# Sparse feed-forward: an expert's second bias is loaded as one row and spread over the partitions by GpSimd, not by the DMA

## What is computed

```python
D, H, E, K, C = 256, 1024, 64, 3, 128          # features, hidden, experts, choices, capacity
def _L0_ffn_ref(x, gate_w, gate_b, w1, b1, w2, b2):
    xf = x.reshape(-1, D)
    logits = xf @ gate_w + gate_b
    top_l, top_i = jax.lax.top_k(logits, K)
    gates = jax.nn.softmax(top_l, axis=-1)
    # each token goes to its 3 experts; an expert keeps its first 128 tokens
    buf = jnp.zeros((E, C, D), x.dtype).at[fe, pos].set(xf[tok], mode='drop')
    h = jax.nn.gelu(jnp.einsum('ecd,edh->ech', buf, w1) + b1[:, None, :], approximate=False)
    y = jnp.einsum('ech,ehd->ecd', h, w2) + b2[:, None, :]
    rows = y[fe, jnp.minimum(pos, C - 1)] * (fg * valid.astype(x.dtype))[:, None]
    return jnp.zeros_like(xf).at[tok].add(rows).reshape(x.shape)

x = x + 0.5 * _L0_ffn_ref(_layernorm(x), ...)   # twice, around attention 0
```

## Time and profile before

| what | us |
|---|---|
| median of 3 runs | 3428.24 (3416.62 to 3428.94) |
| the profiled execution | 3400.82 |
| its span | 3398.8 |
| PE busy | 2905.2 (85%) |
| PE weight load busy | 2080.4 (61%) |
| DVE busy | 1733.6 (51%) |
| ACT busy | 1579.4 (46%) |
| POOL busy | 1286.1 (38%) |
| q1 (SP's DMAs) | 413.98 MB, 47.3% of the 16 engines' span |
| q0 (POOL's DMAs) | 33.57 MB, 4.6% |

### The profile page before, as it was taken

How to read it: one execution, slowest core, us unless ns; L and a number is a source line. 1 busy time by engine, 2 the same in 40 slices (tenths; PEclk the granted TensorE clock), 3 DMA queues, 4 the chain that set the end, 5 groups by cost and what they waited for, 6 DMA issues and landing times. The chain is left out here.

```text
span 3398.8 us, 56446 instructions
## 1 busy us (share of the span) xinstructions
PE 2905.2 (85%) x20629; PEld 2080.4 (61%) x20629; DVE 1733.6 (51%) x4827; ACT 1579.4 (46%) x2598; POOL 1286.1 (38%) x1215
## 2 busy tenths in 40 slices
PE   3599999958999998555999997899859999998997
PEld 3488888823444443345988886566536666665665
DVE  4711111158888788266111111577656666665665
ACT  1133333239988889121333332233237777783332
POOL 3423333359998888043333332000133343320000
PEclk8699999979999999556999999899879999998999
DMA  7179999822554444451999997100066544631001
GB/s 258 44 231 325 317 320 319 264 63 23 59 77 67 58 63 58 49 178 38 296 321 321 315 319 241 37 0 0 19 95 95 81 70 74 90 45 29 0 0 49
DMA packets 368922, 450.78 MB, mean 133 GB/s; under 512 B 87316, under 2 KB 325671, under 8 KB 363559
## 3 DMA queue, kind: packets, MB, share of 16 engines
q1 hardware_dynamic: 344102, 413.98, 47.3%
q0 software_dynamic: 24576, 33.57, 4.6%
HBM read 380.90 MB, written 66.58 MB: 132 GB/s over the span
## 5 line engine op out<-in xcount | busy, mean ns | idle before, releaser
L1542 ACT ACTIVATE f_h_t<-f_h_ps,f_b_t 128x128 f32<-128x128 f32 x1024 | 319.6, 363 | 662.3 <-PE f_h_ps L1501 662.3
L1908 POOL TENSOR_TENSOR a_dmg_buf<-a_c 128x2048 f32<-128x2048 f32 x128 | 520.0, 4087 | 70.8 <-PE a_dmg_ps L1955 45.8
L1501 PEld LDWEIGHTS f_h_ps<-f_rows_t,f_w 128*128 128x128 f32 x4096 | 482.7, 194 | 9.9 <-issue 3.5
L1501 PE MATMUL f_h_ps<-f_rows_t,f_w 128*128 128x128 f32 x4096 | 483.8, 277 | 2.3 <-DVE f_rows_t L1554 1.2
L1512 PE MATMUL f_y_ps<-f_w,f_h_t 128*128 128x256 f32 x2048 | 462.9, 379 | 0.0
L1470 POOL DMA_INDIRECT acc_rows<-f_y,f_give x128 | 203.1, 1587 | 641.7 <-DMA acc_rows<-f_y,f_give 490.1
L1512 PEld LDWEIGHTS f_y_ps<-f_w,f_h_t 128*128 128x128 f32 x2048 | 379.3, 190 | 46.4
L2240 DVE SCALAR_TENSOR_TENSOR a_bond_buf<-a_a,a_small_rep,a_q_ps 128x512 f32<-128x512 f32 x512 | 346.9, 740 | 38.4 <-PE a_bond_ps L1955 36.7
L420 DVE SCALAR_TENSOR_TENSOR f_acc<-f_y_ps,f_gate,f_acc 128x256 f32<-128x256 f32 x576 | 246.5, 479 | 138.0 <-PE f_y_ps L309 132.5
L860 ACT ACTIVATE a_prob<-a_prob,a_neg_top 128x128 f32<-128x128 f32 (+3 forms) x512 | 274.7, 561 | 60.6 <-POOL a_neg_top L674 60.1
L957 DVE CUSTOM_DVE_ANT_0 a_prob<-a_s_ps,a_factor 128x128 f32<-128x128 f32 (+3 forms) x512 | 235.5, 487 | 105.8 <-PE a_s_ps L751 102.4
(11 more groups left out here) (307 smaller groups left out, 4325.8 us busy)
## 6 DMA issues: line engine op xcount, KB each, us to landing
f_w<-in_L_ffn_w_dram SPq DMA_DIRECT2D x256, 1024.0 KB, 7.6
f_b<-in_L_ffn_b_dram SPq DMA_DIRECT2D x128, 128.0 KB, 9.7
a_skewed<-skew SPq DMA_DIRECT2D x8, 2048.0 KB, 8.5
a_q_s<-parts SPq DMA_DIRECT2D x64, 256.0 KB, 10.8
a_k_s<-parts SPq DMA_DIRECT2D x64, 256.0 KB
parts<-a_parts SPq DMA_DIRECT2D x32, 384.0 KB, 7.8
acc_rows<-x_resid SPq DMA_DIRECT2D x17, 512.0 KB, 4.5
xn_rows<-f_xn SPq DMA_DIRECT2D x16, 512.0 KB, 3.1
```

The lines of the kernel that those rows point to most:

```text
L1501: last = nc.tensor.matmul(h_ps[n // HB][:, (n % HB) * P:(n % HB + 1) * P], w1_sb[s][:, c, n * P:(n + 1) * P], rows_t[e % 2][:, c, :], star ...
L1542: nc.scalar.activation(h_t[k][:, n, :], h_ps[n // HB][:, (n % HB) * P:(n % HB + 1) * P], ACT.Gelu, bias=b1_t[:, n, e:e + 1]).then_inc(gelu ...
L1908: nc.gpsimd.tensor_tensor(dmg_buf[n % RING][:, :, :], places(c_sb[h], first_place(dg)), c_sb[h][:, PAD:].unsqueeze(1).broadcast_to([P, DG, ...
```

## The change

SP loads the bias of an expert into one partition, [1, 256]. GpSimd writes it to all 128 partitions with its operation `partition_broadcast`, into one of two buffers [128, 256], one expert ahead of its use. DVE waits for it with a new semaphore, `b2_spread`.

```diff
-        b2_sb = [sb(f"b2_{s}", [P, D]) for s in range(R)]
+        b2_row = [sb(f"b2_row{s}", [1, D]) for s in range(R)]
...
         def load_weights(sp, s, e):
             sp.dma_start(w1_sb[s][:, :, :], w1[e, :, :].rearrange("(c p) h -> p c h", p=P)).then_inc(w_loaded[s], 16)
             sp.dma_start(w2_sb[s][:, :, :], w2[e, :, :].rearrange("(c p) d -> p c d", p=P)).then_inc(w_loaded[s], 16)
-            sp.dma_start(b2_sb[s][:, :], b2[e:e + 1, :].rearrange("o d -> (o d)").partition_broadcast(P)).then_inc(w_loaded[s], 16)
+            sp.dma_start(b2_row[s][:, :], b2[e:e + 1, :]).then_inc(w_loaded[s], 16)
...
+        b2_sb = [sb(f"b2_{k}", [P, D]) for k in range(2)]
...
+            def spread_bias(e):
+                pool.wait_ge(w_loaded[e % R], (e // R + 1) * 48)
+                if e >= 2:
+                    pool.wait_ge(y_copied, e - 1)
+                nc.gpsimd.partition_broadcast(b2_sb[e % 2][:, :], b2_row[e % R][:, :]).then_inc(b2_spread, 1)
+
             for e in range(R):
                 gather(e)
+            spread_bias(0)
             pool.wait_ge(acc_stored, 16 * B)
             for e in range(E):
+                if e + 1 < E:
+                    spread_bias(e + 1)
                 add_rows(e)
                 if e + R < E:
                     gather(e + R)
...
             def finish(e):
                 k = e % 2
                 dve.wait_ge(y_ready, e + 1)
-                nc.vector.tensor_tensor(y_biased[k][:, :], y_ps[k][:, 0:D], b2_sb[e % R][:, :], ALU.add)
+                dve.wait_ge(b2_spread, e + 1)
+                nc.vector.tensor_tensor(y_biased[k][:, :], y_ps[k][:, 0:D], b2_sb[k][:, :], ALU.add)
```

More of the change, by code:

```diff
@@ L1069, in load_weights @@
             sp.dma_start(w2_sb[s][:, :, :], w2[e, :, :].rearrange("(c p) d -> p c d", p=P)).then_inc(w_loaded[s], 16)
-            sp.dma_start(b2_sb[s][:, :], b2[e:e + 1, :].rearrange("o d -> (o d)").partition_broadcast(P)).then_inc(w_loaded[s], 16)
+            sp.dma_start(b2_row[s][:, :], b2[e:e + 1, :]).then_inc(w_loaded[s], 16)
         route(core, sparse, name, gate_w, gate_b, E, b1, b1_rows, b1_loaded, take, give, gate, xn_stored, acc_stored,
               load_weights, R)
-        experts(core, sparse, name, E, H, R, b1_rows, b1_loaded, w1_sb, w2_sb, b2_sb, take, give, gate, acc_stored,
+        experts(core, sparse, name, E, H, R, b1_rows, b1_loaded, w1_sb, w2_sb, b2_row, take, give, gate, acc_stored,
                 w_loaded, load_weights)
@@ L1411, in _, with experts @@
             read_table()
-def experts(core, sparse, name, E, H, R, b1_rows, b1_loaded, w1_sb, w2_sb, b2_sb, take, give, gate, acc_stored,
+def experts(core, sparse, name, E, H, R, b1_rows, b1_loaded, w1_sb, w2_sb, b2_row, take, give, gate, acc_stored,
             w_loaded, load_weights):
@@ L1441, in experts @@
         gelu_done = sem("gelu_done")
+        b2_spread = sem("b2_spread")
         y_ready = sem("e_y_ready")
```

## The result

The changed kernel takes **3378.39 us** (median of 4 runs, 3377.82 to 3381.95), the kernel before 3422.61 in the same series (4 runs, 3416.62 to 3428.94): ratio 0.9873, 95% interval 0.9848 to 0.9898, 44 us or 1.3% faster. The forecast of 3412 was too high by 34 us, and the time lies 6 us under the range.

What follows compares the result with a forecast made beforehand. The expert loop was taken as bound by gathers standing behind weight loads, with PE's 7.24 us as floor. Bias -20, broadcast 0 and switch +3.4 gave -16.6 us: 3412 us from the median 3428.24, range 3384 to 3438.

Steps and rivals of the forecast that it cites:

- What bounds the kernel: Expert loop, two passes: PE waits for late gathers only, 28 times in 55 experts; 7.79 us an expert.
- the floor: Expert loop: PE's own time for an expert, 7.24 us, below which the period cannot fall.
- The 66 us of the prediction: Expert loop: all that cheaper transfers can win, 33 us a pass over 60 experts.
- POOL's transfers behind the load: Expert loop: POOL's small transfers on q0 stand behind a whole load on q1, whose last part is the bias.
- The bias leaves the load: Expert loop: 128 packets fewer, 0.37 us of queue, 0.18 us an expert; 20 us won, bounds 0 and 41.
- the half: Expert loop: shortening a load by d shortens the period by d/2, because the loop spans two experts.
- The count of 55 limited steps: Expert loop: some 55 limited steps a pass, 110 in all, since first four and last few experts are excluded.
- rival 1: Expert loop: the bias counts in full, each scatter landing 0.37 us sooner; 41 us won, 3391 us; chance 0.15.
- The broadcast at nothing: POOL in the expert loop: a broadcast takes 1.26 us, hidden in idle time before scatters; cost 0.
- The switch: GpSimd's code switched around the passes: 6 us each, hidden except 3.4 us exposed at attention 0.
- The base: Whole kernel: gain taken from 3428.24 us, median of runs shown, not the profiled execution's 3400.8.
- Rivals 2, 3 and 4: Nothing won in the loop, 3432 us (0.25); long code switches, slower, 3446 (0.09); slow broadcast bounds POOL, 4068 (0.03).

Runs made afterwards that it cites:

- early_load: Changed kernel with a small IOTA behind each pass's last scatter and SP issuing loads once the down product is done and the row spread: 0.9812, 3356.65 us.
- bias_distinct: Kernel before, but from the fifth expert of each pass the spread bias load is replaced by 128 different 1 KB rows of the second weight: 0.9934.
- w2_less: Kernel before with its spread bias, but from the fifth expert of each pass the last 128 rows of the second weight are not loaded: 0.9904.
- bias_wide: Kernel before, but from the fifth expert of each pass the spread bias load is replaced by 128 KB in 32 rows of 4 KB: 0.9961.
- w_early: Kernel before, but SP issues an expert's two weights once the down product is done, and only the bias waits for VectorE's read: 0.9916.
- first_four: Kernel before, but the spread biases of each pass's first four experts are issued at the end of the route phase, not its head: 0.9979.
- row_plain: Changed kernel without the broadcast on GpSimd; the bias add reads two tiles set to zero once: 0.9858, 3371.07 us.
- bias_twice: Kernel before with the spread bias loaded a second time, into an unread tile, from the fifth expert of each pass: 1.0269, 3513.4 us.
- before_again: Kernel before, unchanged, run for a second profile: 0.999, span 3420.4 us.
- early_again: Changed kernel with one small IOTA into an unread tile behind each pass's last scatter, run beside the changed kernel on one chip: 0.9847, 3374.73 us.
- w2_runs: Changed kernel with small IOTA, second weight laid out as one 8 KB run per partition, first weight read with stride 8: 1.1261, 3855.53 us.

## Why the prediction was wrong, point by point

- **What bounds the kernel: right in the main.** The gather is the only DMA that PE waits for, and 7.24 us is the floor: 28 waits became 8, and early_load with one wait runs at the floor. The 66 us of the prediction are about what is to be had; the changed kernel took 39 us and early_load 59 (966.3 - 906.9).
- **POOL's transfers behind the load: still so.** In the changed kernel a scatter is issued at 403.07 us; from 403.5 to 405.5 all packets are of q1, from 405.5 to 407.5 726 are q1's and 4 q0's, and from 407.5 to 409.5 q0 moves 186:

```profile
q1 hardware_dynamic: 392, 0.77, 100.7%
```

```profile
q1 hardware_dynamic: 726, 0.74, 108.3%
q0 software_dynamic: 4, 0.00, 1.3%
```

```profile
q0 software_dynamic: 186, 0.25, 58.7%
q1 hardware_dynamic: 80, 0.12, 41.0%
```

  The Trainium skill (DMA: Bandwidth & Descriptors, "Queues, rings and completion order") would have them alternate; by these rows they do not, in the changed kernel either. POOL's packets come through as a load runs out.
- **The bias leaves the load: the term that failed.** The sum took 0.37 us of queue and let a step keep half, 0.18 us, 20 us in all; 0.31 us a step was measured, 39.3 us. The picture behind the half was wrong. The prediction saw one load in the period of two experts, "from about 351.0 to 357.0". But SP issues a load in each step, and the first profile shows it in the same stretch:

```profile
340.79 0.37 SPq L1068 DMA_DIRECT2D f_w<-in_L_ffn_w_dram  x1
...
349.27 0.37 SPq L1068 DMA_DIRECT2D f_w<-in_L_ffn_w_dram  x1
...
356.57 0.37 SPq L1068 DMA_DIRECT2D f_w<-in_L_ffn_w_dram  x1
```

  The load issued at 340.79 holds POOL's transfers back as well. The scatter of 344.31 and the gather of 346.21 had been issued; from 345.5 to 348.0 us all packets are q1's, and from 348.5 to 350.5 q0 moves 161:

```profile
q1 hardware_dynamic: 828, 0.92, 107.6%
```

```profile
q0 software_dynamic: 161, 0.22, 49.5%
```

  So two loads stand in the 15.3 us, and both became shorter. Two times 0.37 us, less what the floor of 7.24 cuts off, would give the measured 0.62 us for two steps. That is an argument and not a measurement, for no run times the bias in the queue by itself, and another reading fits too: a spread bias that costs more than 0.37 us, of which a step keeps about half. bias_distinct speaks for it: its 128 different rows cost 0.18 us a step more than the changed kernel (7.54 against 7.36), just what the prediction had taken, and the one row read 128 times adds 0.13. w2_less, with 0.25 us for 128 KB, lies between. Shown is that the term was 0.31 and not 0.18, and that each step has a load of its own; how much of the miss lies in the half and how much in the price of the transfer stays open.
- **The count of 55 limited steps and rival 1.** All 63 intervals of a pass together gave 19.1 and 20.2 us, so the count did little. Rival 1's 41 us come close to the 39.3; it had 0.15. Whether they come about as it said, with each scatter 0.37 us sooner, no run shows. The evidence against it, that PE waits at every second turn only, says where a delay shows and not how many loads it comes from.
- **What the 0.31 us is made of.** Leaving out 128 KB of the second weight gives 0.25 us (w2_less); the row read 128 times costs 0.13 us more than 128 different ones (bias_distinct); packets as such cost little (bias_wide, 0.05). These don't add up exactly; the floor may cut each. The lag ahead of the issue counts too: 0.88 us of it gave 0.19 us a step (w_early), where a full count would have reached the floor.
- **Four biases less in the route phases: not considered, and not settled.** The changed kernel has 2.6 and 1.0 us less there by the table, and first_four 3 to 4 us in the second, but other profiles speak against it (above). The prediction had looked for the transfer's price in the loops alone.
- **The broadcast at nothing: right.** One takes 0.55 us, under the 1.26 us taken; row_plain's steps are the same within 0.02 us, and DVE's idle time before the bias adds did not grow.
- **The switch: size right, exposure unsettled.** 6 us were taken; 5.89 us stood ahead of the first broadcast, 7.70 us ahead of the IOTA, and 9.3 us lay between the bare rows at L267 (2093.8) and its IOTA (2103.1); and PE's first token transposes came at 684.36 - 669.12 = 15.2 us into the phase against 10.1 in the earlier trace rows: 5.1 us later, not 3.4. The figure of the Trainium skill (GPSIMD Engine Reference, "2.1 Instruction dispatch"), about 6 us, is of the same size. In the passes it was hidden, as forecast: the bias add came 8 us after the first broadcast (182.3, 190.4). At L267 the IOTA came at 2103.09 us and DVE read it at 2114.32, so it was hidden there too. The idle 0.25 us that the prediction gives for such rows in before is the one at L98; at L1169 POOL waited for the barrier. What of the 5.1 us reaches the end could not be told.
- **The base.** The profiled execution of before was faster by 20 us in attention 0, as all profiles of one other chip were. Taking the gain from the median of the runs shown (3428.24) was sound in kind; that median itself came down to 3422.61 with a fourth run, 5.6 of the 34 us missed. Most of the rest is the term of the bias (39.3 - 20 = 19 us), then the route phases (3.6 by the table) and the switch, counted at 3.4 and not seen in the times.
- **The range** ended at 41 us of gain from a high median with nothing added for the route phases. Rivals 2, 3 and 4 did not come: the steps moved, a switch took 5.9 to 9.3 us, and a broadcast takes 0.55.

## What to carry to other kernels

Where a load, what waits behind it and the step that issues the next load form a circle, count how many loads flow within one period before halving or doubling a term, from the rows of the engine that issues them; a wait that shows only at every second step does not say it. How much of each saving a step keeps is then still to be measured. And look at what else holds a buffer of the load: once the bias was no longer read out of the load's slot, SP could issue 0.9 us sooner, which brought the loops to the pace of the matmuls.

## What was not expected of the hardware

- A DMA share of 1.01 was not the limit: 330 GB/s went through at 1.02 where 321 had at 1.01.
- 128 reads of one row of 1 KB cost 0.13 us a step more than reads of 128 rows (bias_distinct, 7.67 against 7.54).
- The same transfer was dearer at the head of the load (7.82 us a step) and from ScalarE's queue (8.08) than at its end (7.67).
- With a second spread transfer SP's issues of them took 3.75 and 3.30 us in the median instead of 0.90 (bias_twice, before_again).
- GpSimd's switch showed as idle time behind MODIFY_POOL_CONFIG rows that are short themselves (6 ns ahead of the IOTA, 43 ns ahead of the broadcast): 7.70 us ahead of the IOTA; 7.15 us ahead of the small one in early_again, and 5.89 us ahead of the first broadcast.
- A weight load with a stride of 32 bytes took 335 ns against 194 (w2_runs).
- Attention 0 of one and the same kernel took 769.7 and 790.1 us at a granted clock of 0.96, and the short times go with one chip.
